# State recurrence on three engines: GpSimd multiplies by C for one chunk in four and makes the drives in pairs, with the loops over states written out

## The chip, the cores and the metric

The kernel runs on one core of one Trainium2 chip. The metric is the device time of one execution in microseconds (us), the median of the runs. Engines are named as in the profile: PE is TensorE, PEld its weight loads, DVE is VectorE, ACT is ScalarE, POOL is GpSimd, SP the engine whose queue issues the loads.

## What is computed

The reference is a six-layer stack on x of 32 x 64 tokens by 256 (cross-attention, self-attention, experts, cross-attention, a two-direction Mamba block, a feed-forward). The change lies in the Mamba block. Its recurrence, cut to what matters:

```python
dt = softplus(einsum('blr,dr->bld', dt, Wdt) + bdt)
dA = exp(dt[..., None] * A)                       # decay
dBx = (dt * x)[..., None] * Bm[:, :, None, :]     # drive
def step(hc, inp):                                # over the 64 tokens of a sequence
    dA_t, dBx_t, C_t = inp
    hc = dA_t * hc + dBx_t                        # state, 512 channels x 16 states
    return (hc, einsum('bdn,bn->bd', hc, C_t))    # product with C, summed over the 16 states
y = (ys + x * Dp) * silu(z); out = einsum('bld,ed->ble', y, W_out)
```

It is done for a forward and a reversed direction.

## The kernel before

`project` (stage before) makes x, z, dt, B and C for all 2048 tokens and writes B's rows, and C's rows split into a high and a low part, to DRAM. `recur` then runs 8 passes, numbered 0 to 7: 2 directions (`d`) by 4 blocks (`blk`) of 512 tokens. A pass loops over 16 states `n`, two per iteration of a hardware loop (`Fori`, j = 0, 1), and in each state over CI = 4 chunks `c` of 128 channels. All tiles of a chunk are 128 partitions x 512 tokens in fp32. For one state and chunk:

- SP loads row n of B, broadcast to 128 partitions, into `b_all` (L1653), and row n of C as high and low part into one partition, `c_row` (L1656).
- POOL makes the drive: `drive[c] = b_all * dtx[c]` (L1762), four products of 512 elements per state. It waits until the state's product with C of the same chunk, one state earlier, has been read (`read_done`), since `drive[c]` has one buffer.
- ACT makes the decay `exp(dt * A)` into `decay_ps`, two PSUM buffers (L1745).
- DVE runs the scan `state[c] = decay * state + drive` along the tokens (L1786) and then the product with C, `read[c] = c_ps * state[c]` (L1804). The scan of chunk c+1 is issued ahead of the product of chunk c. `c_ps` is C's row broadcast to 128 partitions in PSUM.
- PE makes `c_ps` by two matmuls with a row of ones (L1669, L1670, `make_c`), and adds `read[c]` to `acc_ps[c]` by a matmul with the identity (L1680); I call it the gather.

Nothing but semaphores orders the engines; each runs its own program in order. Around the loop of a pass, PE makes the dt projection (L1698) once the previous pass's y has been taken from `acc_ps` (L1844 on DVE), ACT makes the softplus (L1726 to L1732), and DVE forms `dt` (L1830) and `dtx = dt * x` (L1833), one chunk after the other, and adds the previous pass's output to x (L1812). Then the first scan starts.

Of the kernel before, what the change touches and what calls it, by code (L numbers as in the profile page):

```python
# [5 lines left out]
F32 = mybir.dt.float32  # L6
# [1383 lines left out]
def mamba(nc, x_sb, ident, a):  # L1390
# [5 lines left out]
    with ExitStack() as ctx:  # L1396
# [20 lines left out]
def project(nc, x_sb, ident, a, zs, xc, xdbl, wx, wdt, wout, vecs, a_log, b_rows, c_rows, dir_in):  # L1417
# [7 lines left out]
    with ExitStack() as ctx:  # L1425
# [157 lines left out]
def recur(nc, ctx, outer_sem, x_sb, ident, zs, xc, xdbl, wdt, wout, vecs, a_log, b_rows, c_rows):  # L1583
# [9 lines left out]
    NCH = NS * CI  # L1593
# [6 lines left out]
    b_all = sb("b_b_all", [P, 2, NB])  # L1600
    c_row = sb("b_c_row", [1, 2, 2, NB], F32R)
# [8 lines left out]
    b_in = [sem(f"b_b_in{j}") for j in range(2)]  # L1610
    c_in = [sem(f"b_c_in{j}") for j in range(2)]
# [12 lines left out]
    read_done = sem("b_read_done")  # L1624
# [19 lines left out]

    @block.sync
# [13 lines left out]

    @block.tensor  # L1660
    def _(pe):
        pe.sem_inc(c_ready, 2)
        pe.wait_ge(const_done, 1)

        def make_c(p, n2, j):

            pe.wait_ge(c_in[j], n2 * 16 + (p * (NS // 2) * 16 + 16))
            pe.wait_ge(read_done, step(p, n2, j, 0) + CI)
            nc.tensor.matmul(c_ps[:, j, :], ones[:, :], c_row[:, j, 0, :], start=True, stop=False)  # L1669
            nc.tensor.matmul(c_ps[:, j, :], ones[:, :], c_row[:, j, 1, :], start=False, stop=True).then_inc(c_ready, 1)  # L1670
# [22 lines left out]
        for p in range(PASSES):  # L1693
# [15 lines left out]
            with pe.Fori(0, NS // 2 - 1) as n2:  # L1709
                states(p, n2, False)  # L1710
# [442 lines left out]
```

## Time and profile before

| | |
|---|---|
| median of 3 runs | 4387.01 us (4385.79 to 4387.67) |
| the profiled execution | 4388.23 us |
| its span | 4386.4 us |
| stretch of the recurrence (3182 to 4204 us) | 1022 us |
| busy in the whole span | PE 3791.6, DVE 2897.2, ACT 1979.2, POOL 1418.0 us |

The profile is of one execution. Times in a row count from the start of the span. A group of instructions shows busy time, mean duration of one, and how long its engine sat idle just before them and who ended that. On DVE the recorded duration of an instruction overlaps a little with the next one's, so what an instruction costs its engine is read from start to start. A run of equal instructions is merged in the view in order of time, with x2 or more behind it.

### The profile page before, as it was taken

The numbers are of one execution on the slowest core, as the hardware profiler recorded it, in microseconds if no ns is written. First come the engines' busy times: TensorE is split into PE (matmuls) and PEld (weight loads), VectorE is DVE, ScalarE is ACT, GpSimd is POOL, SyncE is SP. The second block draws the span as 40 slices with busy tenths as digits, with TensorE's granted clock in tenths as the row PEclk, the third lists the DMA queues.
The fourth block names the chain that finished last, engine by engine and source line by source line (L and its number), as shares of the span: only waits on it lengthen the run. The fifth ranks groups of instructions, "written<-read, shape, count | busy, mean of one in ns | idle before, by whom it ended". The sixth has DMA issues, their size and how long they took to land. (4 is left out here: it accounts for less than half of the span.)

```text
span 4386.4 us, 133964 instructions
## 1 busy us (share of the span) xinstructions
PE 3791.6 (86%) x54334; PEld 2594.8 (59%) x54335; DVE 2897.2 (66%) x4857; ACT 1979.2 (45%) x2986; POOL 1418.0 (32%) x1573
## 2 busy tenths in 40 slices
PE   6999999999797299939999999998877777777778
PEld 4777777777686266627777777776322222222247
DVE  5666666666466122246666666665899999999974
ACT  2555555555433022106555555555444444444432
POOL 3333333333000200052333333331076666667610
PEclk8999999999898599969999999999899999999989
DMA  1010001000002400020000100000011111111100
GB/s 62 25 33 26 26 26 33 26 26 18 9 0 69 185 31 29 30 79 19 32 26 26 33 26 26 26 26 24 12 35 34 32 33 33 32 36 37 32 26 19
DMA packets 61351, 148.44 MB, mean 34 GB/s; under 512 B 8706, under 2 KB 29218, under 8 KB 60482
## 3 DMA queue, kind: packets, MB, share of 16 engines
q1 hardware_dynamic: 57794, 132.75, 9.3%
q8 instruction: 406, 6.65, 0.6%
q0 software_dynamic: 3072, 8.39, 0.6%
q14 instruction: 79, 0.65, 0.0%
HBM read 123.81 MB, written 17.30 MB: 32 GB/s over the span
## 5 line engine op out<-in xcount | busy, mean ns | idle before, releaser
L692 DVE TENSOR_REDUCE x_maxes<-x_misc_ps 128x1 f32<-128x512 f32 (+1 forms) x1792 | 1045.5, 629 | 574.9 <-PE x_misc_ps L476 574.7
L630 ACT ACTIVATE x_probs<-x_score_ps 128x1024 f32<-128x1024 f32 (+1 forms) x896 | 859.5, 961 | 798.7 <-PE x_score_ps L550 792.4
L1762 POOL TENSOR_TENSOR b_drive<-b_b_all,b_dtx 128x512 f32<-128x512 f32 x512 | 653.8, 1278 | 524.9 <-DVE b_dtx L1833 300.6
L1680 PE MATMUL b_acc_ps<-b_read,ident 128*128 128x512 f32 x1024 | 586.4, 660 | 229.8 <-DVE b_read L1804 229.7
L654 POOL CAST x_kT_hi<-x_kT 128x512 fp32r<-128x512 f32 (+1 forms) x448 | 257.7, 575 | 1459.5 <-PE x_misc_ps L494 978.9
L1786 DVE TENSOR_TENSOR_SCAN b_state<-b_decay_ps,b_drive 128x512 f32<-128x512 f32 x512 | 617.0, 1206 | 0.0
L1745 ACT ACTIVATE b_decay_ps<-b_dt,b_a_neg 128x504 f32<-128x504 f32 x512 | 349.8, 684 | 538.5 <-DVE b_state L1786 538.5
L1680 PEld LDWEIGHTS b_acc_ps<-b_read,ident 128*128 128x128 f32 x1024 | 157.4, 193 | 604.8 <-DVE b_read L1804 603.4
L544 PE MATMUL x_score_ps<-x_qz,x_kT 32*128 32x128 f32 x13312 | 496.3, 283 | 10.1 <-ACT x_probs L630 6.2
L526 PE MATMUL x_misc_ps<-x_probs,x_v 128*32 128x64 f32 x26624 | 464.5, 221 | 0.5 <-issue 0.5
L526 PEld LDWEIGHTS x_misc_ps<-x_probs,x_v 128*32 128x32 f32 x26624 | 392.2, 110 | 103.7 <-issue 87.5
L544 PEld LDWEIGHTS x_score_ps<-x_qz,x_kT 32*128 32x128 f32 x13312 | 406.5, 182 | 75.8 <-issue 36.1
L476 PE MATMUL x_misc_ps<-x_kT_hi,x_qz_hi 32*128 32x512 f32 (+1 forms) x2048 | 424.2, 401 | 5.0 <-POOL x_kT_hi L654 4.1
L1804 DVE TENSOR_TENSOR b_read<-b_c_ps,b_state 128x512 f32<-128x512 f32 x512 | 337.0, 659 | 0.0
L604 ACT ACTIVATE x_kT<-x_misc_ps 128x512 f32<-128x512 f32 (+1 forms) x448 | 247.9, 553 | 158.7 <-PE x_misc_ps L463 155.2
L612 ACT ACTIVATE x_v<-x_misc_ps 128x512 f32<-128x512 f32 (+1 forms) x448 | 255.6, 571 | 12.5 <-PE x_misc_ps L494 12.5
L463 PE MATMUL x_misc_ps<-x_raw_hi,x_wk_hi 128*128 128x512 f32 (+1 forms) x512 | 229.8, 449 | 35.2 <-POOL x_raw_lo L369 15.4
L476 PEld LDWEIGHTS x_misc_ps<-x_kT_hi,x_qz_hi 32*128 32x128 f32 x2048 | 208.1, 187 | 83.1 <-DVE x_maxes L692 20.0
L494 PE MATMUL x_misc_ps<-x_wv_hi,x_raw_hi 128*128 128x256 f32 (+1 forms) x832 | 240.9, 290 | 0.3
L369 POOL TENSOR_TENSOR x_raw_lo<-x_raw,x_raw_hi 128x512 fp32r<-128x512 f32 (+1 forms) x192 | 235.0, 1224 | 15.6
L494 PE MATMUL x_misc_ps<-x_wv_lo,x_raw_hi 128*128 128x256 f32 (+1 forms) x832 | 233.7, 281 | 0.0
L494 PE MATMUL x_misc_ps<-x_wv_hi,x_raw_lo 128*128 128x256 f32 (+1 forms) x832 | 233.7, 281 | 0.0
(280 smaller groups left out, 5442.7 us busy)
## 6 DMA issues: line engine op xcount, KB each, us to landing
x_raw<-in_ctxT SPq DMA_DIRECT2D x64, 800.5 KB, 4.4
b_b_all<-b_b_rows SPq DMA_DIRECT2D x128, 256.0 KB, 3.3
m_w<-in_m_w SPq DMA_DIRECT2D x16, 704.0 KB, 19.2
m_w<-in_m_w SPq DMA_DIRECT2D x8, 768.0 KB, 19.8
m_slot_rows<-m_zero SPq DMA_DIRECT2D x1, 4992.0 KB, 17.4
m_block_rows<-m_slot_rows SPq DMA_DIRECT2D x39, 128.0 KB, 2.0
m_slot_out<-m_out SPq DMA_DIRECT2D x39, 128.0 KB, 1.7
x<-in_x SPq DMA_DIRECT2D x1, 2048.0 KB, 8.1
```

The costliest lines, as they stand in the source:

```text
L476: ins = nc.tensor.matmul(dst[:, m * kn:(m + 1) * kn], qz_hi[rows, b % 2, c, :, :].rearrange("p s q -> p (s q)"), kT_hi[rows, (b * NG + n) ...
L494: ins = nc.tensor.matmul(dst[0:keys(i), h * D:(h + 1) * D], part[:, b % 2, cols(i)], w[:, :], start=m == 0, stop=m == 2)
L526: ins = nc.tensor.matmul(dst[j * 32:(j + 1) * 32, r * LQ:(r + 1) * LQ], v_sb[0:keys(i), g, h, 8 * c + 2 * j + half, :], probs[0:keys(i), s ...
L544: nc.tensor.matmul(score_ps[0:kn, j, n * P:(n + 1) * P], kT[rows, u % 2, c, cols(mine[h])], qz[rows, u % 2, c, :, :].rearrange("p s q -> p ...
L630: nc.scalar.activation(probs[rows, s % 2, js, 0:n], score_ps[rows, js, 0:n], ACT.Exp).then_inc(exp_done, 1)
L654: nc.gpsimd.tensor_copy(kT_hi[:, at % 2, 0:m * even].rearrange("p (c k) -> p c k", c=m)[:, :, 0:kn], kT[:, b % 2, c:c + m, k0:k0 + kn]).th ...
L692: nc.vector.tensor_reduce(maxes[:, c:c + m, j, k0 // NB], bank(op)[:, 0:m * even].rearrange("p (c k) -> p c k", c=m)[:, :, 0:kn], AX.X, AL ...
L1680: nc.tensor.matmul(acc_ps[:, c, :], ident[:, :], read[:, c, :], start=False, stop=True, skip_group_check=True).then_inc(acc_done, 1)
L1745: nc.scalar.activation(by_sequence(decay_ps[:, c % 2, :])[:, :, inside(p)], by_sequence(dt[:, c, :])[:, :, inside(p)], ACT.Exp, scale=a_ne ...
L1762: nc.gpsimd.tensor_tensor(drive[:, c, :], b_all[:, j, :], dtx[:, c, :], ALU.mult).then_inc(drive_done, 1)
L1786: nc.vector.tensor_tensor_scan(order(state[:, c, :]), order(decay_ps[:, c % 2, :]), order(drive[:, c, :]), 0.0, ALU.mult, ALU.add).then_in ...
L1804: nc.vector.tensor_tensor(read[:, c, :], c_ps[:, j, :], state[:, c, :], ALU.mult).then_inc(read_done, 1)
```

## The change

1. DVE keeps the scan for all four chunks and the product with C for chunks 0 to 2 (`VE` = 3). POOL makes the product of chunk 3 (`read_last`), from `c_all`, a new tile with C's row broadcast to 128 partitions by a second load (POOL cannot use `c_ps`). For that `project` stores 32 rows (B and C in fp32) where it stored 16.
2. POOL makes the drives two chunks at a time: one instruction of 1024 elements with `b_all` repeated over the two (`make_drive`). The pair waits for the scans of both its chunks one state earlier (`state_done`), no longer for the products. In the first state of a pass it waits for all four `dtx`.
3. SP issues, per state, C's small row first, then B's broadcast, then C's broadcast, each behind a wait of its own.
4. The loops over states are written out on all five engines, and the semaphores count without a head start.

The core of the diff:

```diff
-                    sp.dma_start(b_rows[d, :, tokens], xdbl[R:R + NS, d, tokens]).then_inc(rows_out, 16)
+                    sp.dma_start(bc_rows[d, :, tokens], xdbl[R:, d, tokens]).then_inc(rows_out, 16)
...
+    VE = CI - 1
...
+    c_all = sb("b_c_all", [P, 2, NB])
...
     def _(sp):
-        for p in range(PASSES):
-            d, blk = direction(p)
-            with sp.Fori(0, NS // 2) as n2:
-                for j in range(2):
-                    state_rows = ds(n2 * 2 + j, 1)
-                    sp.wait_ge(drive_done, step(p, n2, j, 0) + CI)
-                    sp.dma_start(b_all[:, j, :], b_rows[d, state_rows, tokens(p)].rearrange("n t -> (n t)")
-                                 .partition_broadcast(P)).then_inc(b_in[j], 16)
-                    sp.wait_ge(c_ready, n2 * 2 + (p * NS + j + 1))
-                    sp.dma_start(c_row[:, j, :, :].bitcast(F32),
-                                 c_rows[d, :, state_rows, tokens(p)].rearrange("i n t -> n i t")
-                                 ).then_inc(c_in[j], 16)
+        for k, (p, n) in enumerate(STATES):
+            d = direction(p)[0]
+            if k >= 2:
+                sp.wait_ge(c_ready, k - 1)
+            sp.dma_start(c_row[:, k % 2, :, :].bitcast(F32), c_rows[d, :, n:n + 1, tokens(p)].rearrange("i n t -> n i t")
+                         ).then_inc(c_in[k % 2], 16)
+            if k >= 2:
+                sp.wait_ge(drive_done, (k - 1) * CI)
+            sp.dma_start(b_all[:, k % 2, :], bc_rows[d, n:n + 1, tokens(p)].rearrange("n t -> (n t)")
+                         .partition_broadcast(P)).then_inc(b_in[k % 2], 16)
+            if k >= 2:
+                sp.wait_ge(pool_read_done, k - 1)
+            sp.dma_start(c_all[:, k % 2, :], bc_rows[d, NS + n:NS + n + 1, tokens(p)].rearrange("n t -> (n t)")
+                         .partition_broadcast(P)).then_inc(c_all_in[k % 2], 16)
...
-        def make_c(p, n2, j):
-
-            pe.wait_ge(c_in[j], n2 * 16 + (p * (NS // 2) * 16 + 16))
-            pe.wait_ge(read_done, step(p, n2, j, 0) + CI)
-            nc.tensor.matmul(c_ps[:, j, :], ones[:, :], c_row[:, j, 0, :], start=True, stop=False)
-            nc.tensor.matmul(c_ps[:, j, :], ones[:, :], c_row[:, j, 1, :], start=False, stop=True).then_inc(c_ready, 1)
...
-                for c in range(CI):
-                    pe.wait_ge(read_done, step(p, n2, j, c) + 2 * CI + 1)
-                    nc.tensor.matmul(acc_ps[:, c, :], ident[:, :], read[:, c, :], start=False, stop=True,
-                                     skip_group_check=True).then_inc(acc_done, 1)
+        def make_c(k):
+            pe.wait_ge(c_in[k % 2], k // 2 * 16 + 16)
+            if k >= 2:
+                pe.wait_ge(ve_read_done, (k - 1) * VE)
+            nc.tensor.matmul(c_ps[:, k % 2, :], ones[:, :], c_row[:, k % 2, 0, :], start=True, stop=False)
+            nc.tensor.matmul(c_ps[:, k % 2, :], ones[:, :], c_row[:, k % 2, 1, :], start=False, stop=True).then_inc(c_ready, 1)
+
+        def gather(k, c):
+            if c < VE:
+                pe.wait_ge(ve_read_done, k * VE + c + 1)
+            else:
+                pe.wait_ge(pool_read_done, k + 1)
+            nc.tensor.matmul(acc_ps[:, c, :], ident[:, :], read[:, c, :], start=False, stop=True,
+                             skip_group_check=True).then_inc(acc_done, 1)
...
-        pool.sem_inc(drive_done, 2 * CI)
+        def make_drive(k, c):
+
+            if k > 0:
+                pool.wait_ge(state_done, (k - 1) * CI + c + 2)
+            nc.gpsimd.tensor_tensor(drive[:, c:c + 2, :], b_all[:, k % 2:k % 2 + 1, :].broadcast_to([P, 2, NB]),
+                                    dtx[:, c:c + 2, :], ALU.mult).then_inc(drive_done, 2)
+
+        def read_last(k):
+            pool.wait_ge(c_all_in[k % 2], k // 2 * 16 + 16)
+            pool.wait_ge(state_done, k * CI + CI)
+            if k > 0:
+                pool.wait_ge(acc_done, k * CI)
+            nc.gpsimd.tensor_tensor(read[:, VE, :], c_all[:, k % 2, :], state[:, VE, :], ALU.mult).then_inc(pool_read_done, 1)
+
         for p in range(PASSES):
-            with pool.Fori(0, NS // 2) as n2:
-                for j in range(2):
-                    for c in range(CI):
-                        if c == 0:
-                            pool.wait_ge(b_in[j], n2 * 16 + (p * (NS // 2) * 16 + 16))
-                        if j == 0:
-                            pool.wait_ge(dtx_done, p * CI + c + 1)
-
-                        pool.wait_ge(read_done, step(p, n2, j, c) + CI + 1)
-                        nc.gpsimd.tensor_tensor(drive[:, c, :], b_all[:, j, :], dtx[:, c, :], ALU.mult
-                                                ).then_inc(drive_done, 1)
+            for n in range(NS):
+                k = p * NS + n
+                pool.wait_ge(b_in[k % 2], k // 2 * 16 + 16)
+                if n == 0:
+                    pool.wait_ge(dtx_done, p * CI + CI)
+                for c in range(0, CI, 2):
+                    make_drive(k, c)
+                if n > 0:
+                    read_last(k - 1)
+            read_last(p * NS + NS - 1)
...
-        def scan(p, n2, j, c):
-            k = step(p, n2, j, c)
-            dve.wait_ge(drive_done, k + 2 * CI + 1)
-            dve.wait_ge(decay_done, k + 1)
+        def scan(p, n, c):
+            k = p * NS + n
+            dve.wait_ge(drive_done, k * CI + c // 2 * 2 + 2)
+            dve.wait_ge(decay_done, k * CI + c + 1)
+            if c == VE and k > 0:
+                dve.wait_ge(pool_read_done, k)
 
...
-        def states(p, n2, last):
-            for j in range(2):
-                for c in range(CI):
-                    k = step(p, n2, j, c)
-
-                    if c < CI - 1:
-                        scan(p, n2, j, c + 1)
-                    elif j == 0:
-                        scan(p, n2, 1, 0)
-                    elif not last:
-                        scan(p, n2 + 1, 0, 0)
-                    dve.wait_ge(state_done, k + 3)
-                    dve.wait_ge(acc_done, k + 1)
-                    if c == 0:
-                        dve.wait_ge(c_ready, n2 * 2 + (p * NS + j + 3))
-                    nc.vector.tensor_tensor(read[:, c, :], c_ps[:, j, :], state[:, c, :], ALU.mult
-                                            ).then_inc(read_done, 1)
+        def read_chunk(p, n, c):
+            k = p * NS + n
+            dve.wait_ge(state_done, k * CI + c + 1)
+            if k > 0:
+                dve.wait_ge(acc_done, (k - 1) * CI + c + 1)
+            if c == 0:
+                dve.wait_ge(c_ready, k + 1)
+            nc.vector.tensor_tensor(read[:, c, :], c_ps[:, k % 2, :], state[:, c, :], ALU.mult).then_inc(ve_read_done, 1)
...
-            scan(p, 0, 0, 0)
-            with dve.Fori(0, NS // 2 - 1) as n2:
-                states(p, n2, False)
-            states(p, NS // 2 - 1, True)
+            scan(p, 0, 0)
+            for n in range(NS):
+                for c in range(CI):
+                    if c < CI - 1:
+                        scan(p, n, c + 1)
+                    elif n < NS - 1:
+                        scan(p, n + 1, 0)
+                    if c < VE:
+                        read_chunk(p, n, c)
```

DVE, the inner part of a pass. Before, a scan and a product alternate (the row's operation name SCALAR_TENSOR_TENSOR is the scan); these are the last five rows of a pass:

```order
L1804 TENSOR_TENSOR b_read<-b_c_ps,b_state 128x512
L1786 SCALAR_TENSOR_TENSOR b_state<-b_decay_ps,b_drive 128x512
L1804 TENSOR_TENSOR b_read<-b_c_ps,b_state 128x512
L1786 SCALAR_TENSOR_TENSOR b_state<-b_decay_ps,b_drive 128x512
L1804 TENSOR_TENSOR b_read<-b_c_ps,b_state 128x512 x2
```

After, ten rows from the middle of a pass:

```order
L1809 TENSOR_TENSOR b_read<-b_c_ps,b_state 128x512
L1799 SCALAR_TENSOR_TENSOR b_state<-b_decay_ps,b_drive 128x512 x2
L1809 TENSOR_TENSOR b_read<-b_c_ps,b_state 128x512
L1799 SCALAR_TENSOR_TENSOR b_state<-b_decay_ps,b_drive 128x512
L1809 TENSOR_TENSOR b_read<-b_c_ps,b_state 128x512
L1799 SCALAR_TENSOR_TENSOR b_state<-b_decay_ps,b_drive 128x512
L1809 TENSOR_TENSOR b_read<-b_c_ps,b_state 128x512
L1799 SCALAR_TENSOR_TENSOR b_state<-b_decay_ps,b_drive 128x512 x2
L1809 TENSOR_TENSOR b_read<-b_c_ps,b_state 128x512
L1799 SCALAR_TENSOR_TENSOR b_state<-b_decay_ps,b_drive 128x512
```

Before, every scan has a product behind it. After, the product of chunk 3 is missing, so once in a state two scans stand behind each other (x2).

POOL, before, the end of the body of its loop (eight products in two states) with its register instructions:

```order
L1762 TENSOR_TENSOR b_drive<-b_b_all,b_dtx 128x512
L1761 REGISTER_ALU
L1762 TENSOR_TENSOR b_drive<-b_b_all,b_dtx 128x512
L1761 REGISTER_ALU
L1762 TENSOR_TENSOR b_drive<-b_b_all,b_dtx 128x512
L1753 REGISTER_ALU
L1753 COMPARE_AND_BRANCH
```

After:

```order
L1765 TENSOR_TENSOR b_read<-b_c_all,b_state 128x512
L1757 TENSOR_TENSOR b_drive<-b_b_all,b_dtx 128x1024 x2
L1765 TENSOR_TENSOR b_read<-b_c_all,b_state 128x512
L1757 TENSOR_TENSOR b_drive<-b_b_all,b_dtx 128x1024 x2
L1765 TENSOR_TENSOR b_read<-b_c_all,b_state 128x512
```

Four products of 512 became two of 1024, and the product of the state before stands behind both. The product of the last chunk is therefore made after the next state's second pair of drives.

SP, before, the second half of its loop, and after, two states:

```order
L1653 ISA
L1653 DMA b_b_all<-b_b_rows 128x512
L1655 REGISTER_ALU
L1656 DMA b_c_row<-b_c_rows 1x2x512
L1649 REGISTER_ALU
```

```order
L1652 DMA b_c_row<-b_c_rows 1x2x512
L1656 DMA b_b_all<-b_bc_rows 128x512
L1660 DMA b_c_all<-b_bc_rows 128x512
L1652 DMA b_c_row<-b_c_rows 1x2x512
L1656 DMA b_b_all<-b_bc_rows 128x512
L1660 DMA b_c_all<-b_bc_rows 128x512
```

There is one more broadcast load per state, and the small row of C moved from last to first.

## Rows read from the trace of the kernel before

**Rows 1.** Busy time by engine in the recurrence's stretch (count), granted clock, DMA.
```profile
3182.00:4204.00 1022.00, 772.47 (x1652) 265.58 (x1650) 982.92 (x1166) 421.41 (x624) 653.81 (x512) 0.97 0.12 33
```

**Rows 2.** Groups by line, steady stretch of pass 2: busy us, mean ns, idle before.
```profile
L1762 POOL TENSOR_TENSOR b_drive<-b_b_all,b_dtx 128x512 f32<-128x512 f32 x36 | 45.4, 1262 | 16.2 <-DVE b_read L1804 16.2
L1786 DVE TENSOR_TENSOR_SCAN b_state<-b_decay_ps,b_drive 128x512 f32<-128x512 f32 x36 | 43.4, 1206 | 0.0
L1680 PE MATMUL b_acc_ps<-b_read,ident 128*128 128x512 f32 x71 | 40.0, 644 | 15.3 <-DVE b_read L1804 15.3
L1745 ACT ACTIVATE b_decay_ps<-b_dt,b_a_neg 128x504 f32<-128x504 f32 x35 | 24.0, 685 | 36.0 <-DVE b_state L1786 36.0
L1804 DVE TENSOR_TENSOR b_read<-b_c_ps,b_state 128x512 f32<-128x512 f32 x35 | 23.1, 659 | 0.0
...
L1669 PE MATMUL b_c_ps<-b_c_row,b_ones 1*128 1x512 f32 x9 | 4.5, 497 | 0.0
```

**Rows 3.** VectorE in order of time, one state: start us, duration us.
```profile
3453.42 1.21 DVE L1786 TENSOR_TENSOR_SCAN b_state<-b_decay_ps,b_drive 128x512 f32<-128x512 f32 x1
3454.55 0.66 DVE L1804 TENSOR_TENSOR b_read<-b_c_ps,b_state 128x512 f32<-128x512 f32 x1
3455.13 1.21 DVE L1786 TENSOR_TENSOR_SCAN b_state<-b_decay_ps,b_drive 128x512 f32<-128x512 f32 x1
...
3460.27 1.21 DVE L1786 TENSOR_TENSOR_SCAN b_state<-b_decay_ps,b_drive 128x512 f32<-128x512 f32 x1
```

**Rows 4.** Who waited for whom, 3470 to 3540 us: total us, times, longest.
```profile
POOL b_drive L1762 <- DVE b_read L1804: 18.9, 42, 0.5
```

**Rows 5.** Groups by shape on GpSimd, whole run: busy us, mean ns.
```profile
L369 POOL TENSOR_TENSOR x_raw_lo<-x_raw,x_raw_hi 128x512 fp32r<-128x512 f32 x128 | 151.2, 1181 | 10.4
L369 POOL TENSOR_TENSOR x_raw_lo<-x_raw,x_raw_hi 128x577 fp32r<-128x577 f32 x64 | 83.8, 1310 | 5.2
...
L639 POOL TENSOR_TENSOR x_qz<-x_qT,x_mask 128x256 f32<-128x256 f32 x64 | 39.3, 615 | 0.0
...
L378 POOL TENSOR_TENSOR x_wk_lo<-x_wk,x_wk_hi 128x256 fp32r<-128x256 f32 x2 | 1.4, 720 | 0.2
```

**Rows 6.** VectorE in order of time at the start of pass 1.
```profile
3309.52 1.29 DVE L1830 TENSOR_TENSOR b_dt<-b_dt,b_dtx 128x512 f32<-128x512 f32 x2 [3.33 <-ACT b_dtx L1732]
3310.74 0.69 DVE L1833 TENSOR_TENSOR b_dtx<-b_dt,b_xc 128x512 f32<-128x512 f32 x1
...
3311.94 1.76 DVE L1833 TENSOR_TENSOR b_dtx<-b_dt,b_xc 128x512 f32<-128x512 f32 x1
...
3316.50 1.28 DVE L1812 TENSOR_TENSOR x<-b_c_ps,x 128x512 f32<-128x512 f32 x2
3317.70 2.32 DVE L1786 TENSOR_TENSOR_SCAN b_state<-b_decay_ps,b_drive 128x512 f32<-128x512 f32 x2
```

**Rows 7.** GpSimd in order of time at the start of pass 1.
```profile
3311.65 1.50 POOL L1762 TENSOR_TENSOR b_drive<-b_b_all,b_dtx 128x512 f32<-128x512 f32 x1 [16.43 <-DVE b_dtx L1833]
...
3316.13 2.80 POOL L1762 TENSOR_TENSOR b_drive<-b_b_all,b_dtx 128x512 f32<-128x512 f32 x2 [0.71 <-DVE b_dtx L1833]
```

**Rows 8.** VectorE in order of time at the end of pass 1.
```profile
3424.99 1.21 DVE L1786 TENSOR_TENSOR_SCAN b_state<-b_decay_ps,b_drive 128x512 f32<-128x512 f32 x1
3426.12 1.26 DVE L1804 TENSOR_TENSOR b_read<-b_c_ps,b_state 128x512 f32<-128x512 f32 x2
```

**Rows 9.** TensorE in order of time at the end of pass 1.
```profile
3426.83 1.98 PE L1680 MATMUL b_acc_ps<-b_read,ident 128*128 128x512 f32 x4 [0.59 <-DVE b_read L1804]
3428.75 0.69 PE L1698 MATMUL b_acc_ps<-b_xdbl,b_wdt 64*128 64x512 f32 x1
```

**Rows 10.** Line 1680 in two stretches of pass 2: busy (count), granted clock.
```profile
3445.10:3451.80 6.70, 3.39 (x4) 1.00 (x4) 0.50 0.16 40
3452.00:3458.80 6.80, 4.45 (x10) 1.14 (x10) 1.00 0.19 42
```

**Rows 11.** DMA issues by line, 3470 to 3540 us: KB each, us to landing.
```profile
b_b_all<-b_b_rows SPq DMA_DIRECT2D x10, 256.0 KB, 3.3
```

More of the change, by code:

```diff
@@ L1592, in recur @@
     TPH = TPB // 2
-    NCH = NS * CI
+    VE = CI - 1
     a_neg = sb("b_a_neg", [P, 2, CI, NS])
@@ L1610, in recur @@
     b_in = [sem(f"b_b_in{j}") for j in range(2)]
+    c_all_in = [sem(f"b_c_all_in{j}") for j in range(2)]
     c_in = [sem(f"b_c_in{j}") for j in range(2)]
@@ L1623, in recur @@
     state_done = sem("b_state_done")
-    read_done = sem("b_read_done")
+    ve_read_done = sem("b_ve_read_done")
+    pool_read_done = sem("b_pool_read_done")
     acc_done = sem("b_acc_done")
@@ L1707, in _ @@
                 pe.wait_ge(x_done, p * 2)
-            make_c(p, 0, 0)
-            with pe.Fori(0, NS // 2 - 1) as n2:
-                states(p, n2, False)
-            states(p, NS // 2 - 1, True)
+            make_c(p * NS)
+            for n in range(NS):
+                k = p * NS + n
+                if n < NS - 1:
+                    make_c(k + 1)
+                for c in range(CI):
+                    gather(k, c)
         pe.wait_ge(y_done, PASSES * CI)
@@ L1737, in _ @@
             act.wait_ge(edge_done, d + 1)
-            with act.Fori(0, NS // 2) as n2:
-                for j in range(2):
-                    for c in range(CI):
-                        if j == 0:
-                            act.wait_ge(dt_done, p * CI + c + 1)
-                        act.wait_ge(state_done, step(p, n2, j, c) + 1)
-                        nc.scalar.activation(by_sequence(decay_ps[:, c % 2, :])[:, :, inside(p)],
-                                             by_sequence(dt[:, c, :])[:, :, inside(p)], ACT.Exp,
-                                             scale=a_neg[:, d, c, ds(n2 * 2 + j, 1)]).then_inc(decay_done, 1)
+            for n in range(NS):
+                for c in range(CI):
+                    q = (p * NS + n) * CI + c
+                    if n == 0:
+                        act.wait_ge(dt_done, p * CI + c + 1)
+                    if q >= 2:
+                        act.wait_ge(state_done, q - 1)
+                    nc.scalar.activation(by_sequence(decay_ps[:, c % 2, :])[:, :, inside(p)],
+                                         by_sequence(dt[:, c, :])[:, :, inside(p)], ACT.Exp,
+                                         scale=a_neg[:, d, c, n:n + 1]).then_inc(decay_done, 1)
@@ L1787, in scan @@
                                          0.0, ALU.mult, ALU.add).then_inc(state_done, 1)
-        def states(p, n2, last):
-            for j in range(2):
-                for c in range(CI):
-                    k = step(p, n2, j, c)
-                    if c < CI - 1:
-                        scan(p, n2, j, c + 1)
-                    elif j == 0:
-                        scan(p, n2, 1, 0)
-                    elif not last:
-                        scan(p, n2 + 1, 0, 0)
-                    dve.wait_ge(state_done, k + 3)
-                    dve.wait_ge(acc_done, k + 1)
-                    if c == 0:
-                        dve.wait_ge(c_ready, n2 * 2 + (p * NS + j + 3))
-                    nc.vector.tensor_tensor(read[:, c, :], c_ps[:, j, :], state[:, c, :], ALU.mult
-                                            ).then_inc(read_done, 1)
+        def read_chunk(p, n, c):
+            k = p * NS + n
+            dve.wait_ge(state_done, k * CI + c + 1)
[4 more added lines that the diff above has]
+            nc.vector.tensor_tensor(read[:, c, :], c_ps[:, k % 2, :], state[:, c, :], ALU.mult).then_inc(ve_read_done, 1)
         def add_output(p):
@@ L1836, in _ @@
                 add_output(p - 1)
-            scan(p, 0, 0, 0)
-            with dve.Fori(0, NS // 2 - 1) as n2:
-                states(p, n2, False)
-            states(p, NS // 2 - 1, True)
+            scan(p, 0, 0)
+            for n in range(NS):
+                for c in range(CI):
+                    if c < CI - 1:
[4 more added lines that the diff above has]
+                        read_chunk(p, n, c)
             for c in range(CI):
-                dve.wait_ge(acc_done, (p + 1) * NCH + c + 1)
+                dve.wait_ge(acc_done, ((p + 1) * NS - 1) * CI + c + 1)
                 nc.vector.tensor_tensor(xc[:, d, c, tokens(p)], acc_ps[:, c, :], zs[:, c, tokens(p)], ALU.mult
```

25 lines of the change are left out of this document (9 added, 16 removed).

## The prediction

> **What bounds the kernel now.** I read the busy time by stretch first. The recurrence takes 1022 of the 4386.4 us, and in it DVE is busy for 983 us, PE 772, POOL 654, ACT 421, with TensorE's granted clock at 0.97 [rows 1]. Nothing outside this stretch changes but eight stores in `project`. Then the groups by line inside a pass: DVE's two lines have no idle time before them, every other engine idles and names DVE or waits for what DVE released [rows 2], and POOL waits for DVE's product 42 times in 70 us [rows 4]. In order of time, a scan is followed by its product after 1.13 us (3453.42 to 3454.55), the next scan comes 0.58 us later (3455.13), and a state of four such pairs takes 3460.27 - 3453.42 = 6.85 us [rows 3]. DVE never waits inside a pass, so a state's time is the sum of DVE's issue distances. The last product and the first y of the pass keep the same rhythm [rows 8].
>
> **What the change removes.** One product of four leaves DVE, which is 0.58 us per state, by its distance and not by its 0.66 us of duration. Where two scans stand behind each other the distance is again one scan's: two take 2.32 us, less one of 1.21 is 1.11 [rows 6]; I use 1.13. A state then costs DVE 6.85 - 0.58 = 6.27 us. From the first scan of a pass to its last there are 15 such products, 15 x 0.58 = 8.7 us, in 8 passes 69.9 us (with 0.583, since the two products of 1.26 us lie 1.26 - 0.68 = 0.58 apart [rows 8]). The 16th is worked out below.
>
> **What it puts on POOL.** A product of 512 takes 1.26 us [rows 2]. No row shows one of 1024. The nearest are the same operation with plain rows: 0.72 us for 256 elements [rows 5] and 1.26 for 512, so 0.54 more per 256, and 1024 would take 1.26 + 1.08 = 2.35 us. The low end is the step from 512 to 577 elements of L369, 0.129 us for 65 [rows 5], which gives 1.26 + 1.02 = 2.28. The high end starts from 0.615 for 256, the only row with a repeated operand [rows 5], and gives 1.26 + 1.30 = 2.56; doubling gives 2.52. I take 2.35, because L378 is the closest in form. POOL's state is then 2 x 2.35 + 1.26 = 5.96 us, plus about 0.1 us to pick up the scan it waits for, against DVE's 6.27. Back-to-back products add no gap: two take 2.80, with a first of about 1.56 [rows 7]. So POOL stays hidden, but with only 0.2 to 0.3 us of cover; from a pair of 2.50 on, POOL sets the pace, and each further 0.1 us of the pair costs 0.2 us x 120 states = 24 us.
>
> The Trainium skill speaks against the move: "GPSIMD Engine Reference", section "Elementwise, side-by-side cycle accounting", calls the Vector engine the rule for elementwise work, GpSimd being about twice as slow. The trace agrees on the ratio, 1262 to 659 ns [rows 2]. By the rule the moved product costs more work than it saves; it would cost time only if POOL ended last, which is rival B.
>
> **Who waits for whom after it.** Let T be the end of the scan of chunk 3. POOL starts the second drive pair of the next state at T+0.1, has it at T+2.4, the product of chunk 3 at T+3.7, the next first pair at T+6.1. DVE needs them as follows. After that scan it has a product, scan 0, scan 1, product 0, then scan 2: it starts at T-0.08+0.58+1.13+1.13+0.58 = T+3.3, 0.9 us after the second pair. Scan 3, which now also waits until POOL has read `state[3]`, starts at T+5.1, 1.4 us after. Scan 0 of the state after needs the next first pair at T+6.8, 0.7 us after. The decays, 0.69 us each on ACT [rows 2], follow a scan by two places and have at least 1.7 us. On PE the gather of chunk 3 moves to T+3.8, and behind it in order stand the next `c_ps` and the gathers of the next state. PE's state is 8 matmuls of 0.644 and two of about 0.5 [rows 2], 6.1 us at most by durations, which overlap. The product that needs this gather comes a state later. DMA: one more load of 256 KB per state, 3.3 us to landing [rows 11]. SP's queue is in order, so B's load of state k+1 stands behind C's load of state k, which waits for the product of state k-2. That frees at T+3.7 and the data is wanted more than 8 us later, even at twice 3.3 us. SP's second wait per load, the wider store in `project` (8 times, 64 KB for 32) and the written-out loops I set at nothing: the first two are covered by that slack or lie among other stores. The loop ends cost nothing now either, since 63 scans of a pass take 3424.99 - 3317.70 = 107.29 us [rows 6, 8], which is 62 x 1.712 + 1.13.
>
> **Pass ends.** The last scan is followed now by two products, and the last gather starts when the gather before it leaves PE (four matmuls in 1.98 us from 3426.83, then L1698 at 3428.75 [rows 9]). After, POOL's product ends 1.21 + 0.1 + 1.26 = 2.57 us after the scan's start at 3424.99, at 3427.56, and PE is free at about 3427.8. The next pass's chain runs over PE (L1698), so the 16th product saves nothing there: 0, between -0.3 and +0.3 per pass.
>
> **Pass starts.** Now POOL's first drives run against DVE's `dtx`: the product at 3311.94 takes 1.76 us where the first took 0.69, and POOL's take 1.50 to 1.57 for 1.26 [rows 6, 7]. After the change POOL waits for all four `dtx`, so the eight DVE products run undisturbed at 0.605 us (3309.52 to 3311.94 for four): the last starts at 3309.52 + 7 x 0.605 = 3313.76 and ends at 3314.44. POOL picks up 0.23 us later (3310.74 + 0.69 to 3311.65 [rows 6, 7]), has the pair at 3317.0, and the scan starts at 3317.1 for 3317.70: 0.6 us earlier in 7 passes. In the first pass no addition to x (1.2 us) stands between, so it starts 0.6 us later. Net 7 x 0.6 - 0.6 = 3.6 us earlier. With a pair of 2.56 it is 2.3, with 2.28 it is 4.0. The Trainium skill has this contention ("GPSIMD Engine Reference", "Specifications": DVE instructions with two SBUF inputs share GpSimd's interfaces), and rows 6 agree. By the same rule scans and C products, with one PSUM input, stay at 1.21 and 0.66 us under a busier POOL, as rows 2 show for a POOL at 74%.
>
> **Sum.** 69.9 + 3.6 = 73.5 us off the profiled execution's 4388.23, which is 4314.7. That execution lies 1.2 us over the median, so 4313.5 us.
>
> **Rivals.**
> - A, forecast, 0.71: DVE stays the bound, 4313.5; its own range is 4308 to 4320 (the pass ends by 8 x 0.3, the pair's ends, a little of a state lost where a pass begins).
> - B, 0.18: POOL becomes the bound. For it speaks the cover of 0.2 us, against it rows 5. With a pair of 2.56 a state takes 2 x 2.56 + 1.26 = 6.38, with a tenth for waits 6.48: 6.85 - 6.48 = 0.37 x 120 = 44, plus 2, so 4341. Between 4320 and 4345.
> - C, 0.05, slower: POOL's pair costs over 2.79 us, since from there 2 pairs and 1.26 exceed 6.85. That is the case if all of POOL's products run as at pass starts (1.56 [rows 7], a pair 3.1): 2 x 3.1 + 1.26 = 7.46, (7.46 - 6.85) x 120 = 73 us slower, 4460. Against it: in rows 2 the drives lie beside scans and products all the time at 1.262 us.
> - D, 0.03: the gather of chunk 3 comes late, PE then idles some 1.6 us per state and works in bursts, and its clock falls. At 0.50 four matmuls of L1680 kept PE busy 3.39 us, at 1.00 ten took 4.45 [rows 10]. A state wholly at the low level, 8 x 0.85 and two of about 0.85, is 8.5 us, 1.65 x 120 = 198 slower (4585); falling for a part of the time it hides. Against it, the clock is 1.00 now with PE idle between all gathers.
> - E, 0.03: the straight-line code or SP's chained waits stall DVE by about what is saved, 0.58 us per state, and the time stays at 4387.
>
> **How the numbers follow.** A measurement here tells 0.2%, 9 us, from no change. A and B are faster, C and D slower, E the same: faster 0.89, same 0.03, slower 0.08. The range for 8 in 10 takes A's and the greater part of B: 4306 to 4338.
>
> **What the new profile would show.** In a pass, the distance of two scans of chunk 0 is 6.27 us, with two scans 1.13 apart once in it, and no idle time on DVE's lines; POOL's pair at 2.35 us and some 0.2 us idle per state before a drive whose releaser is the scan; PE's gather of chunk 3 right after POOL's product; `dtx` products all at 0.69 us; first to last scan of a pass 98.5 us. The prediction is wrong if DVE's scan idles with a drive as its releaser (B or C), if L1680's matmuls average over 0.8 us (D), or if idle time without a releaser appears on DVE (E).

## The result and the profile after

The changed kernel takes 4310.39 us (median of 4 runs, 4308.34 to 4312.86), the one before, measured beside it, 4387.34 (4385.79 to 4388.63). The ratio is 0.9825, 95% interval 0.9808 to 0.9842. The profiled execution of after has a span of 4308.7 us; line numbers below are of the changed kernel: L1799 is the scan, L1809 DVE's product with C, L1757 a pair of drives, L1765 POOL's product with C, L1679 the gather, L1747 the decay.

The recurrence by engine, as in [rows 1] (PE, PEld, DVE, ACT, POOL, clock, DMA share, GB/s), over nearly its whole stretch:

```profile
3170.00:4190.00 1020.00, 810.96 (x1843) 338.37 (x1843) 941.00 (x1139) 453.56 (x678) 755.03 (x384) 0.91 0.24 69
```

POOL is now at 755 us of 1020, the clock at 0.91 for 0.97, the DMA traffic doubled. Groups by line in a steady stretch (3480 to 3530 us), to hold against [rows 2]:

```profile
L1799 DVE TENSOR_TENSOR_SCAN b_state<-b_decay_ps,b_drive 128x512 f32<-128x512 f32 x28 | 33.2, 1205 | 0.0
L1679 PE MATMUL b_acc_ps<-b_read,ident 128*128 128x512 f32 x60 | 31.2, 645 | 10.5 <-POOL b_read L1765 10.2 <-DVE b_read L1809 0.3
L1757 POOL TENSOR_TENSOR b_drive<-b_b_all,b_dtx 128x1024 f32<-128x1024 f32 x13 | 30.6, 2353 | 2.5 <-DVE b_state L1799 2.5
L1747 ACT ACTIVATE b_decay_ps<-b_dt,b_a_neg 128x504 f32<-128x504 f32 x26 | 17.8, 685 | 22.5 <-DVE b_state L1799 22.5
L1809 DVE TENSOR_TENSOR b_read<-b_c_ps,b_state 128x512 f32<-128x512 f32 x21 | 13.9, 661 | 0.0
...
L1765 POOL TENSOR_TENSOR b_read<-b_c_all,b_state 128x512 f32<-128x512 f32 x8 | 10.1, 1268 | 2.7 <-DVE b_state L1799 2.7
...
L1671 PE MATMUL b_c_ps<-b_c_row,b_ones 1*128 1x512 f32 x6 | 3.0, 495 | 0.0
```

DVE's two lines still have no idle time before them. In order of time, DVE in one state, against [rows 3]:

```profile
3452.32 1.21 DVE L1799 TENSOR_TENSOR_SCAN b_state<-b_decay_ps,b_drive 128x512 f32<-128x512 f32 x1
3453.45 0.66 DVE L1809 TENSOR_TENSOR b_read<-b_c_ps,b_state 128x512 f32<-128x512 f32 x1
3454.03 2.33 DVE L1799 TENSOR_TENSOR_SCAN b_state<-b_decay_ps,b_drive 128x512 f32<-128x512 f32 x2
3456.28 0.66 DVE L1809 TENSOR_TENSOR b_read<-b_c_ps,b_state 128x512 f32<-128x512 f32 x1
3456.86 1.21 DVE L1799 TENSOR_TENSOR_SCAN b_state<-b_decay_ps,b_drive 128x512 f32<-128x512 f32 x1
...
3458.57 1.21 DVE L1799 TENSOR_TENSOR_SCAN b_state<-b_decay_ps,b_drive 128x512 f32<-128x512 f32 x1
...
3460.28 1.21 DVE L1799 TENSOR_TENSOR_SCAN b_state<-b_decay_ps,b_drive 128x512 f32<-128x512 f32 x1
```

Two scans stand together (3454.03, 2.33 us), and from 3454.03 to 3460.28 a state takes 6.25 us, where it took 6.85. POOL in the same state:

```profile
3453.67 2.35 POOL L1757 TENSOR_TENSOR b_drive<-b_b_all,b_dtx 128x1024 f32<-128x1024 f32 x1 [0.36 <-DVE b_state L1799]
3455.98 1.27 POOL L1765 TENSOR_TENSOR b_read<-b_c_all,b_state 128x512 f32<-128x512 f32 x1
3457.21 2.35 POOL L1757 TENSOR_TENSOR b_drive<-b_b_all,b_dtx 128x1024 f32<-128x1024 f32 x1
3459.93 2.35 POOL L1757 TENSOR_TENSOR b_drive<-b_b_all,b_dtx 128x1024 f32<-128x1024 f32 x1 [0.36 <-DVE b_state L1799]
```

From start to start a state of POOL is 2.31 (3453.67 to 3455.98), 1.23 and then 2.72 us, of which 0.36 is the wait for the scan. What POOL needs is 2.31 + 1.23 + 2.36 = 5.9 us; it waits for DVE, not DVE for it. A gather is two matmuls in the trace. PE makes the three gathers of DVE's products in a row (the six matmuls at 3452.77), and then waits 1.69 us for POOL's product before the last one (the two at 3457.31):

```profile
3452.77 2.84 PE L1679 MATMUL b_acc_ps<-b_read,ident 128*128 128x512 f32 x6
3457.31 1.13 PE L1679 MATMUL b_acc_ps<-b_read,ident 128*128 128x512 f32 x2 [1.69 <-POOL b_read L1765]
```

The start of pass 1, DVE against [rows 6] and POOL's first two pairs against [rows 7]:

```profile
3297.08 1.29 DVE L1834 TENSOR_TENSOR b_dt<-b_dt,b_dtx 128x512 f32<-128x512 f32 x2 [3.33 <-ACT b_dtx L1734]
...
3300.70 1.28 DVE L1837 TENSOR_TENSOR b_dtx<-b_dt,b_xc 128x512 f32<-128x512 f32 x2
3301.90 1.28 DVE L1816 TENSOR_TENSOR x<-b_c_ps,x 128x512 f32<-128x512 f32 x2
3304.60 2.34 DVE L1799 TENSOR_TENSOR_SCAN b_state<-b_decay_ps,b_drive 128x512 f32<-128x512 f32 x2 [1.42 <-POOL b_drive L1757]
```
```profile
3302.21 4.65 POOL L1757 TENSOR_TENSOR b_drive<-b_b_all,b_dtx 128x1024 f32<-128x1024 f32 x2 [14.83 <-DVE b_dtx L1837]
```

All four `dtx` run undisturbed, the first pair starts when they are done, and DVE idles 1.42 us for it. SP, about the loads of two states:

```profile
3345.37 0.33 SPq L1660 DMA_DIRECT2D b_c_all<-b_bc_rows  x1
3345.74 0.58 SPq L1652 DMA_DIRECT2D b_c_row<-b_c_rows  x1
3346.36 0.40 SPq L1656 DMA_DIRECT2D b_b_all<-b_bc_rows  x1
3351.61 0.33 SPq L1660 DMA_DIRECT2D b_c_all<-b_bc_rows  x1
```

C's broadcast waits for POOL's product two states back; the small row of the next state is issued right behind it.

### The profile page after: what moved, and what is told of

Same layout as the page of the kernel before. It is cut to its first block and busy times, and to the rows that moved or that the text cites. A ratio compares the mean times of both kernels' runs of the same rounds, so it can differ in the third digit from the quotient of the medians.

```text
span 4308.7 us, 129527 instructions
## 1 busy us (share of the span) xinstructions
PE 3776.3 (88%) x54334; PEld 2632.0 (61%) x54335; DVE 2804.7 (65%) x4729; ACT 1979.2 (46%) x2986; POOL 1519.9 (35%) x1445
## 5 line engine op out<-in xcount | busy, mean ns | idle before, releaser
L1679 PE MATMUL b_acc_ps<-b_read,ident 128*128 128x512 f32 x1024 | 566.1, 683 | 187.3 <-POOL b_read L1765 153.8
L1757 POOL TENSOR_TENSOR b_drive<-b_b_all,b_dtx 128x1024 f32<-128x1024 f32 x256 | 602.5, 2354 | 331.2 <-DVE b_dtx L1837 280.7
L1799 DVE TENSOR_TENSOR_SCAN b_state<-b_decay_ps,b_drive 128x512 f32<-128x512 f32 x512 | 606.7, 1205 | 12.5 <-POOL b_drive L1757 12.5
L1747 ACT ACTIVATE b_decay_ps<-b_dt,b_a_neg 128x504 f32<-128x504 f32 x512 | 350.0, 685 | 461.9 <-DVE b_state L1799 461.9
L1679 PEld LDWEIGHTS b_acc_ps<-b_read,ident 128*128 128x128 f32 x1024 | 193.9, 211 | 505.9 <-POOL b_read L1765 257.2
L1809 DVE TENSOR_TENSOR b_read<-b_c_ps,b_state 128x512 f32<-128x512 f32 x384 | 253.7, 661 | 0.0
```

The costliest lines, as they stand in the source:

```text
L1747: nc.scalar.activation(by_sequence(decay_ps[:, c % 2, :])[:, :, inside(p)], by_sequence(dt[:, c, :])[:, :, inside(p)], ACT.Exp, scale=a_ne ...
L1757: nc.gpsimd.tensor_tensor(drive[:, c:c + 2, :], b_all[:, k % 2:k % 2 + 1, :].broadcast_to([P, 2, NB]), dtx[:, c:c + 2, :], ALU.mult).then_ ...
L1799: nc.vector.tensor_tensor_scan(order(state[:, c, :]), order(decay_ps[:, c % 2, :]), order(drive[:, c, :]), 0.0, ALU.mult, ALU.add).then_in ...
```

## The experiments

Each run was measured beside the kernel before, whose medians were 4386.9, 4385.06 and 4386.25 us on three chips. A "state" is the distance of two scans of chunk 0 inside a pass.

**Nothing but the loops written out.** The kernel before with `for n2 in range(...)` for each `Fori`:

```diff
-            with dve.Fori(0, NS // 2 - 1) as n2:
+            for n2 in range(NS // 2 - 1):
```

> The kernel before with nothing changed but the loops over states written out on all five engines. Theory (loop ends and register instructions lie under VectorE's products): 1.71 us a chunk as before, 4387 within 2 us. Rival (loop ends cost time): some us faster; the other rival (straight-line code stalls an engine): slower, with idle time on VectorE.

Measured: 4387.31 us, ratio 1.0001 (0.9991 to 1.001), and a state of 6.85 us as before. Within that interval the loops cost nothing and the written-out code costs nothing.

**Everything but the moved product.**

```diff
-    VE = CI - 1
+    VE = CI
...
-            sp.dma_start(c_all[:, k % 2, :], ...
...
-                    read_last(k - 1)
-            read_last(p * NS + NS - 1)
```

> The changed kernel with all four products with C back on VectorE and without the third load; drives in pairs, loops written out and C's small row first are kept. Theory (only the moved product shortens the state): 6.85 us a state, and the pass starts keep their 0.6 us in 7 passes less 0.6 in the first, so 4387.3 - 3.6 = 4384 us, ratio 0.999. Rival (pairs, written-out loops or the load order bring a share of the gain): under 4375 us, with a state under 6.8 us.

Measured: 4382.19 us, ratio 0.9992 (0.9982 to 1.0001). A state is 6.85 us; the stretch from the first `dt` of a pass to its first scan is 7.53 us for 8.17, the same as in the changed kernel. So the state is shortened by the moved product alone. The shorter pass starts come from the pairs' wait for all `dtx`: the run with the first pair on the first two `dtx`, below, is back at 8.18 us.

**Single drives.**

```diff
-            nc.gpsimd.tensor_tensor(drive[:, c:c + 2, :], b_all[...].broadcast_to([P, 2, NB]), dtx[:, c:c + 2, :], ...
+            nc.gpsimd.tensor_tensor(drive[:, c, :], b_all[:, k % 2, :], dtx[:, c, :], ...
```

> The changed kernel with the drives made one chunk at a time again, each waiting for its own scan of the state before; the moved product stays on GpSimd. Theory (the state is the larger of VectorE's 6.25 us and GpSimd's sum): GpSimd's state is 5 products of 1.265 us = 6.33 us and sets the pace, 6.33 to 6.40 us a state, so (6.35 - 6.25) x 120 = about 12 us over the changed kernel's 4310, less about 1 us per pass start since the first drive is ready 1.1 us sooner: 4310 to 4318, with VectorE's scan idle behind a drive in every state. Rival (pairing has no bearing, GpSimd's cover is wide): 6.25 us a state, no idle time on VectorE within a pass, 4301 to 4303.

Measured: 4304.52 us (4300.63 to 4308.76), ratio 0.9813 (0.9797 to 0.983). The theory was wrong here and the rival right. POOL in order of time:

```profile
3452.28 1.26 POOL L1764 TENSOR_TENSOR b_read<-b_c_all,b_state 128x512 f32<-128x512 f32 x1
3453.51 4.94 POOL L1757 TENSOR_TENSOR b_drive<-b_b_all,b_dtx 128x512 f32<-128x512 f32 x4
3458.42 1.26 POOL L1764 TENSOR_TENSOR b_read<-b_c_all,b_state 128x512 f32<-128x512 f32 x1
```

Five products take 4.94 us for four (3453.51 to 3458.42 is 4.91) and 1.23 for the fifth, 6.14 us in all, although each is recorded at 1.26: on POOL too one starts some 0.04 us before the end recorded for the one before it. 6.14 fits under 6.25, so pairing the drives was not needed for the gain. It costs about 6 us, at the pass starts; the medians alone, 4304.52 and 4310.39, lie closer than the 9 us that tell a difference here, and it is the trace that shows it: the first scan comes 6.34 us after the first `dt` in each pass, where the changed kernel has 7.53.

**Single drives in the first state of a pass only.**

```diff
+            if k % NS == 0:
+                for i in (c, c + 1):
+                    nc.gpsimd.tensor_tensor(drive[:, i, :], b_all[:, k % 2, :], dtx[:, i, :], ALU.mult).then_inc(drive_done, 1)
+                return
```

> The changed kernel, but in the first state of each pass the four drives are made singly, after all four dtx as in it. Theory (each pass start waits for the first pair, 2.35 us, on VectorE): the first scan starts 1.09 us sooner; scan 1 then waits some 0.15 us for its drive at 1.26 us a drive, so about 0.9 to 1.0 us per pass, 7 to 8 us in 8 passes: 4302 to 4303.5 us, first to last scan of a pass 98.4 to 98.6 us. Rival (something else holds the first scan, the products' matmul or the decay): no change, 4310.

Measured: 4303.29 us (4302.71 to 4304.22), ratio 0.9808 (0.9792 to 0.9825). DVE at the start of pass 1:

```profile
3301.88 1.28 DVE L1820 TENSOR_TENSOR x<-b_c_ps,x 128x512 f32<-128x512 f32 x2
3303.40 2.46 DVE L1803 TENSOR_TENSOR_SCAN b_state<-b_decay_ps,b_drive 128x512 f32<-128x512 f32 x2 [0.24 <-POOL b_drive L1759]
```

The idle time before the first scan falls from 1.42 to 0.24 us; the first scan comes 6.34 us after the first `dt` for 7.53, and first to last scan takes 98.45 for 98.33, which leaves 1.07 us per pass.

**More work on POOL.** One further product per state in 15 of 16 states, of constants into a spare tile that nobody reads, 256 elements and 512:

```diff
+                    if c == 0 and n > 0:
+                        nc.gpsimd.tensor_tensor(spare[...], diag[:, 0, ...], diag[:, 1, ...], ALU.mult).then_inc(spare_done, 1)
```

> The changed kernel with one more GpSimd product of 256 elements per state (constants into a spare tile, read by nobody) between the two pairs of drives, in 15 of 16 states. Theory (a state costs the larger of VectorE's 6.25 us and GpSimd's sum of start-to-start distances, 2 x 2.31 + 1.22 = 5.85 in the changed kernel): the extra one is 0.72 less the 0.04 of overlap, 0.68, so GpSimd's sum is 6.53 and a state 6.53 to 6.6: 0.28 to 0.35 x 120 = 34 to 42 us over the changed kernel, 4344 to 4352. Rival (GpSimd is not near the bound): 4310 and 6.25 us a state.

> The same with 512 elements. Theory: GpSimd's sum is 5.85 + 1.22 = 7.07 us a state, more than the 6.85 of the kernel before: 0.82 x 120 = 98 us over the changed kernel, 4408, slower than before by 0.5%. Rival (GpSimd is not near the bound, or only its wait for the scan counts): under 4370.

Measured: 4343.5 us, ratio 0.99 (0.9884 to 0.9917), and 4401.78 us, ratio 1.0038 (1.0024 to 1.0053). With 256 the states settle at 6.53 to 6.54 us, after four or five at 6.25 in which POOL uses up its lead; with 512 they settle at 7.07 to 7.08. That is 5.85 us (2 x 2.31 + 1.23) and one more distance of 0.68 or 1.23, as expected; both medians came out a little under the times expected. Two of the groups by line, 3480 to 3550 us, of the second kernel, the scan, which now idles behind a pair of drives, and the further product:

```profile
L1807 DVE TENSOR_TENSOR_SCAN b_state<-b_decay_ps,b_drive 128x512 f32<-128x512 f32 x40 | 47.7, 1215 | 6.2 <-POOL b_drive L1759 5.9
...
L1782 POOL TENSOR_TENSOR b_spare<-b_diag 128x512 f32<-128x512 f32 x10 | 12.5, 1254 | 0.0
```

So a state costs the larger of two sums, and the sum on POOL is made of start-to-start distances. The second kernel is slower than the kernel before, as rival C had it from 6.85 us of POOL on.

**C's small row last.**

```diff
-            if k >= 2:
-                sp.wait_ge(c_ready, k - 1)
-            sp.dma_start(c_row[...], ...)          # moved behind the load of c_all
```

> The changed kernel with C's small row issued last in each state, behind both broadcasts, as the kernel before had it behind B's. Theory (all three loads are ready well over a microsecond before they are wanted): 4310 within 2 us, 6.25 us a state. Rival (the small row behind C's broadcast, which waits for GpSimd's product two states back, makes c_ps late): VectorE's first product of a state idles behind TensorE's pair for c_ps, and the time is over 4315.

Measured: 4355.93 us, ratio 0.9932 (0.9916 to 0.9949): more than half of the gain is gone, the theory was wrong and the rival right. Who waited for whom in pass 5:

```profile
PE b_c_ps L1671 <- DMA b_c_row<-b_c_rows: 23.9, 11, 3.1
...
DVE b_read L1809 <- PE b_acc_ps L1679: 7.8, 7, 2.2
```

In order of time, one state, with POOL, SP's queue, PE and DVE:

```profile
3841.41 1.26 POOL L1765 TENSOR_TENSOR b_read<-b_c_all,b_state 128x512 f32<-128x512 f32 x1
...
3842.69 0.33 SPq L1656 DMA_DIRECT2D b_c_all<-b_bc_rows  x1
...
3843.07 0.56 SPq L1660 DMA_DIRECT2D b_c_row<-b_c_rows  x1
...
3846.77 0.49 PE L1671 MATMUL b_c_ps<-b_c_row,b_ones 1*128 1x512 f32 x1 [1.96 <-DMA b_c_row<-b_c_rows]
...
3848.64 0.69 DVE L1809 TENSOR_TENSOR b_read<-b_c_ps,b_state 128x512 f32<-128x512 f32 x1
```

POOL's product ends at 3842.67, SP issues C's broadcast at 3842.69 and the row at 3843.07, and PE's pair for `c_ps` starts at 3846.77, 3.7 us after the issue. That pair stands in PE's program ahead of the gathers of the state before, DVE has gone on, and its next product waits for a gather.

The lateness is not the same everywhere. Two rows of pass 1, in the forward direction:

```profile
3350.49 0.57 SPq L1660 DMA_DIRECT2D b_c_row<-b_c_rows  x1
3353.21 0.50 PE L1671 MATMUL b_c_ps<-b_c_row,b_ones 1*128 1x512 f32 x1 [1.94 <-DMA b_c_row<-b_c_rows]
```

Here it is 2.7 us from issue to pair. Over the rows that PE sat idle for, 9 or 10 in a pass, the median is 2.6 us in passes 0 to 3 and 3.7 in passes 4 to 7. Taken from the end of POOL's product the pair then comes at 3.0 or 4.1 us, where the changed kernel has it at 1.1. First to last scan takes 100.1 to 100.9 us in the forward passes and 104.5 to 107.9 in the reversed ones, for 98.33. In the forward passes every state over 6.3 us lies on a stretch at 1.2 GHz or right behind one; at 2.4 GHz PE made up for the late row. In the reversed passes states are longer at 2.4 GHz too. So 8 us of the loss came from a late row and a low clock together, and 33 us in the passes where the row is later still; the rest lies mostly at the pass ends. The low clock alone costs nothing: the next run has as many low stretches as the changed kernel and its time.

**The same with three buffers for C's broadcast.**

```diff
-            if k >= 2:
-                sp.wait_ge(pool_read_done, k - 1)
-            sp.dma_start(c_all[:, k % 2, :], ...
+            if k >= 3:
+                sp.wait_ge(pool_read_done, k - 2)
+            sp.dma_start(c_all[:, k % 3, :], ...
```

> The kernel with C's small row last (4356 us), and only the broadcast of C given three buffers for two, so that its load waits for GpSimd's product three states back. Theory (the small row was late because it stood behind the wait for the product two states back, 3.0 us late per state): the row is issued one state, 6.25 us, earlier and lands 3 us ahead of its use; 4310 within 3 us, 6.25 us a state, no wait of TensorE for the row's load. Rival (the row is late because 512 KB of broadcasts stand before it in the DMA queues): still over 4340 with the same waits.

Measured: 4311.68 us, ratio 0.9832 (0.9815 to 0.9848), states of 6.25 us, and no wait of PE for the row. The row is as far behind the two broadcasts in the queue as before; what made it late was the wait in front of it. With that wait gone, the place of the row no longer matters.

**No load of C's broadcast.**

```diff
             if k >= 2:
-                sp.wait_ge(pool_read_done, k - 1)
+                continue
...
-            pool.wait_ge(c_all_in[k % 2], k // 2 * 16 + 16)
+            pool.wait_ge(c_all_in[k % 2], 16)
```

> The changed kernel without the broadcast load of C but in the first two states, so that GpSimd's product uses stale rows of C (the loads of 126 states are left out, and the output is that of stale rows for one chunk in four). Theory (the third load is hidden): 4310 within 2 us, 6.25 us a state. Rival (32 MB more of DMA slows some engine): over 5 us faster.

Measured: 4310.57 us (4308.44 to 4312.04), states of 6.25 us. The kernel leaves out 126 of the 128 broadcasts of C, and gains nothing by it: the third load is free.

**First pair on the first two dtx.**

```diff
-                    pool.wait_ge(dtx_done, p * CI + CI)
+                        pool.wait_ge(dtx_done, p * CI + c + 2)   # before each pair of the first state
```

> The changed kernel, but the first pair of drives of a pass waits for the first two dtx only, the second for all four. Theory (GpSimd and VectorE contend while both read two SBUF tensors): dtx and dt products beside the pair stretch from 0.69 towards 1.8 us as at the pass starts of the kernel before, and the pair past 2.6; the pair would start some 2.2 us earlier but VectorE's four products behind it end about 1.5 to 2 us later, and the additions to x follow them, so the first scan starts 0 to 1.0 us sooner than in the changed kernel: 4302 to 4310. Rival (no contention, the rows of before had another reason): the products stay at 0.69, the pair is ready before VectorE is, and the first scan starts 1.4 us sooner: 4299.

Measured: 4314.18 us (4312.57 to 4316.06), outside the range given, and not faster than the changed kernel. DVE, then POOL:

```profile
3299.02 0.69 DVE L1834 TENSOR_TENSOR b_dt<-b_dt,b_dtx 128x512 f32<-128x512 f32 x1
3299.62 3.44 DVE L1837 TENSOR_TENSOR b_dtx<-b_dt,b_xc 128x512 f32<-128x512 f32 x2
3302.98 1.28 DVE L1816 TENSOR_TENSOR x<-b_c_ps,x 128x512 f32<-128x512 f32 x2
3304.18 2.32 DVE L1799 TENSOR_TENSOR_SCAN b_state<-b_decay_ps,b_drive 128x512 f32<-128x512 f32 x2
```
```profile
3299.33 2.58 POOL L1757 TENSOR_TENSOR b_drive<-b_b_all,b_dtx 128x1024 f32<-128x1024 f32 x1 [13.02 <-DVE b_dtx L1837]
```

The first scan comes 8.18 us after the first `dt`, 0.65 later than in the changed kernel. The product of chunk 2 was to take 0.60 us and with the next one takes 3.44 in all. POOL's pair ends at 3301.91; 3303.06, the end of the two, is 1.15 later, which is two products of 0.55 to 0.6. So DVE's product did not run slowly beside POOL's instruction, it stood until that one was over. [rows 6, 7] read the same way: POOL's drive ended at 3313.15, and DVE's product of 1.76 us 0.55 later. I had expected a stretch in proportion, and so undersized it for an instruction twice as long.

The Trainium skill ("SBUF — State Buffer", section "Who interferes with whom") calls contention for the ports that the two engines share an exclusive lock, and counts VectorE instructions with two SBUF inputs among what contends with GpSimd's reads. That the one issued first keeps the ports for its whole instruction, it says of VectorE's two-port modes. The trace shows it for a product of two SBUF inputs as well, with 2.8 us for 0.69; and POOL's own 0.23 us more fit it, since it began at 3299.33 inside DVE's product of 3299.02.

**A version that goes further.** Single drives, and DVE's products of chunks 0 and 1 in one instruction behind the scan of chunk 2:

```diff
+            if c == 1:
+                nc.vector.tensor_tensor(read[:, 0:2, :], c_ps[:, k % 2:k % 2 + 1, :].broadcast_to([P, 2, NB]),
+                                        state[:, 0:2, :], ALU.mult).then_inc(ve_read_done, 2)
+                return
```

> The changed kernel with single drives (as in the run with single drives, 4304.5 us) and VectorE's products of chunks 0 and 1 in one instruction of 1024 elements, behind the scan of chunk 2. Theory (VectorE's issue distances are 512 or 1024 elements at 0.96 GHz-like 1.04 ns and some 0.05 us per instruction): one distance of 1.12 for two of 0.583, a state 6.20 to 6.22 for 6.25, so 4 to 6 us under 4304.5: 4298 to 4300. Rival (GpSimd, whose five products take 5 x 1.225 = 6.13 us plus the pick-up of a scan, becomes the bound): 6.25 or more, 4304 or more.

Measured: 4296.44 us (4294.0 to 4297.7), ratio 0.9797 (0.978 to 0.9813), states of 6.19 us. The theory held, and the time came out a little below its range. It has the lowest median of all, 14 us under the changed kernel: 6 are those of the single drives (4304.52), and the states give about 7 (0.06 x 120), 98.49 to 97.66 us from first to last scan, on the mean of the passes, against the run with single drives. GpSimd's sum, 6.14 us, is now 0.05 under VectorE's.

## Why the prediction was right, step by step

- **The bound and the removed product.** DVE stayed the bound inside a pass (A). A state was predicted at 6.27 us and is 6.25; first to last scan takes 98.33 for 98.5. The 0.02 lies in the first product behind two scans, which comes after 1.11 us and not 1.13. That makes 71.6 us in 8 passes for 69.9.
- **POOL's pair.** Predicted 2.35 us, mean 2.354 in 256 of them. The value is right, but the cover behind it was mis-sized: I summed durations (5.96 + 0.1) where distances count (5.85, or 5.9 with the pick-up of the scan). I put the pair at which POOL sets the pace at 2.50 us; by distances, (6.25 - 1.23) / 2 + 0.04, my estimate is now 2.55. The same slip made my theory of the single drives wrong.
- **Pass ends.** Predicted 0; from the last scan to the first `dt` of the next pass it is 12.30 us before and after.
- **Pass starts.** Predicted 0.6 us sooner in 7 passes and 0.6 later in the first; measured 8.17 to 7.53 from the first `dt`, 0.65 sooner, and 20.72 to 21.20 us from the block's first product of constants, 0.48 later.
- **Outside the recurrence.** In the spans the sum is 71.6 + 7 x 0.65 - 0.5 = 75.6 us. The rest of 77.7 lies in the code in front of the recurrence (4.0 us shorter) and behind it (1.8 longer), and is no part of the forecast. That first product of constants starts between 3163.5 and 3168.6 us in the 11 kernels with the wider stores, and at 3166.7 and 3169.2 in the two with the old ones, so it is not shown that the stores matter. I forecast 73.5; the median moved by 77.0.
- **SP's queue, set at nothing.** Its result held, its reason did not cover the small row. I gave the slack of the two broadcasts, over 8 us, and had no price for the row, whose pair on PE stands ahead of the gathers of the state before and is wanted about 1.1 us after POOL's product ends. With two buffers for C's broadcast, fetching the row first is what hides it: last, it costs 45.5 us (4355.93 to 4310.39). Of the parts of the change, this one carries the most after the moved product.
- **Rivals.** B and C did not come about, but exist at their price, as the two runs with more POOL work show. D's mechanism did come about in part: in the recurrence the granted clock falls to 1.2 GHz in 30 short stretches for 8 before, and the stretch's mean to 0.91. Before, all 8 lay at the pass starts ([rows 10] show one); now 22 lie further inside the passes. Ahead of 18 of them TensorE had worked in bursts with one idle stretch of 1.6 to 2.0 us per state; ahead of the other 4 stood the longer idle stretch of a pass start, 3.2 us. So my argument against D, that PE idles between all gathers and keeps its clock, did not carry over. What kept D's price away is PE's slack: a matmul of L1679 averages 1.10 us in the low stretches and 0.62 outside them, and yet no state but one is longer. E fell with the written-out loops.

Open: why the small row arrives 1.1 us later in the four passes of the reversed direction, and what moves the code in front by some us from kernel to kernel.

## What to carry to other kernels

- When work is moved from the bound engine to one with idle time, compare sums of start-to-start distances per iteration on both; the durations of a trace overlap and hide some of the cover.
- A queue served in order needs its loads sorted by when they are wanted, counted from the place at which the consumer's own program takes them, and not only by the size of their slack: one wait in front of a 4 KB row was worth 45 us here, and one more buffer behind that wait was worth the same.
- Keep VectorE's instructions with two SBUF inputs away from GpSimd's long ones. With one operand in PSUM they ran side by side at full speed.

## What the runs showed of the hardware

- A VectorE product of two SBUF tensors that meets a GpSimd product waits until that is over: 1.76 us beside one of 1.50, 2.8 us beside a pair of 2.58, for 0.69 alone. GpSimd's own, where it begins inside such a product, is lengthened by 0.23 to 0.31 us (1.50 to 1.57 for 1.26, 2.58 for 2.35). With one operand in PSUM, VectorE's scans and products stayed at 1.21 and 0.66 us.
- GpSimd's products follow each other after 1.23 us (512 elements) and 2.31 us (1024), for recorded durations of 1.26 and 2.354.
- A 4 KB row issued between two broadcasts of 256 KB reached its reader 2.6 us after its issue in four passes and 3.7 us in the other four (medians of the run with the row last).
- The broadcasts of C doubled the traffic, from 33 to 69 GB/s, at no cost that shows: 4310.57 us without them and 4310.39 with them.
- TensorE's granted clock fell to 1.2 GHz 18 times in the steady part of the passes, where TensorE's idle stretches just before lasted 1.6 to 2.0 us, one per state. With the gathers spread over the state, before the change, it did not fall there.
